# Gates' weights scaled once, router logits from the transposed halves, a third FFN tile ahead: one change to a recurrent block with experts

## What is computed

```python
xn = _layernorm(x, axis=-1)
# _L0_attn_ref(xn):
h = _rmsnorm(xn, pre_norm_w)
a = sigmoid(h @ w_a + decay_bias)
i_gate = sigmoid(h @ w_i)
v = h @ w_v
input_signal = sqrt(clip(1.0 - a * a, 1e-08)) * (i_gate * v)
rec_out = _chunked_scan(a, input_signal)      # state = a * state + signal along the sequence
x1 = xn + rec_out @ out_proj_w
gate, up = split(_rmsnorm(x1, ffn_norm_w) @ w_gate_up, 2, axis=-1)
attn = x1 + silu(gate) * up @ w_down
# _L0_ffn_ref(xn): logits = xn @ w_router, the best two of 8 experts per token,
# softmax over the two, y = square(relu(xn @ w_fc[e])) @ w_proj[e], weighted sum
out = x + attn + moe
```

## Time and profile before

| | us |
|---|---|
| median of 3 runs (312.35 to 313.71) | 312.52 |
| profiled execution, its own time | 313.96 |
| span of the profiled execution, first to last instruction | 312.2 |
| TensorE busy | 288.3 (92%) |
| VectorE busy | 194.6 (62%) |
| ScalarE busy | 174.7 (56%) |
| GpSimd busy | 145.6 (47%) |

### The profile page before, as it was taken

How to read it: one execution, slowest core, us unless ns; L and a number is a source line. 1 busy time by engine, 2 the same in 40 slices (tenths; PEclk the granted TensorE clock), 3 DMA queues, 4 the chain that set the end, 5 groups by cost and what they waited for, 6 DMA issues and landing times.

```text
span 312.2 us, 5645 instructions
## 1 busy us (share of the span) xinstructions
PE 288.3 (92%) x1842; PEld 255.1 (82%) x1842; DVE 194.6 (62%) x467; ACT 174.7 (56%) x360; POOL 145.6 (47%) x129
## 2 busy tenths in 40 slices
PE   5599799997999969999998999899999999799993
PEld 5578688886898949889997989789988999688882
DVE  2486998799867767874555588645546555612323
ACT  2587596798657744553657545346566555423220
POOL 4633001003174013576686678656766666637400
PEclk9799979998999999999999999999999999979999
DMA  7999940005996000244344434243444444539998
GB/s 225 325 381 378 457 174 0 0 2 149 205 200 131 0 11 26 46 64 74 62 71 68 59 64 68 54 70 52 70 69 70 68 69 57 66 34 134 195 197 285
DMA packets 33356, 36.92 MB, mean 118 GB/s; under 512 B 5168, under 2 KB 30512, under 8 KB 33296
## 3 DMA queue, kind: packets, MB, share of 16 engines
q0 software_dynamic: 13840, 17.20, 34.8%
q1 hardware_dynamic: 16560, 17.25, 16.3%
q10 hardware_dynamic: 2928, 2.10, 2.1%
HBM read 24.68 MB, written 13.96 MB: 124 GB/s over the span
## 4 chain that ended last, share of the span: by engine, by line
PE 74%; DVE 10%; ACT 8%; issue 4%; DMA 2%; SPq 0%; DVEq 0%; ACTq 0%
PE ps L364 61%; PE ps L425 5%; PE ps L571 5%; DMA Waiv_raw<-in_L_attn_w_v_dram 2%; ACT h L735 2%; DVE at_lane L1068 1%; PE ps L373 1%; PE ps L390 1%; DVE gu L1109 1%; DVE h2T_lo L986 1%; DVE hT_lo L937 1%; ACT Wpj_hi L670 1%; ACT h2T_hi L743 1%; DVE X L1122 1%; DVE Wpj_lo L1104 1%
## 5 line engine op out<-in xcount | busy, mean ns | idle before, releaser
L1339 POOL DMA_INDIRECT xg<-xh_dram,gather_u x39 | 46.2, 1185 | 56.7 <-DVE picks L1139 47.5
L1348 POOL DMA_INDIRECT acc_dram<-yb,gather_u x39 | 62.4, 1599 | 16.0 <-issue 8.6
L364 PE MATMUL ps<-h2T_lo,Wgu_hi 128*128 128x512 f32 x128 | 43.5, 400 | 0.0
L364 PE MATMUL ps<-h2T_hi,Wgu_hi 128*128 128x512 f32 x128 | 41.6, 407 | 1.0 <-DVE h2T_lo L986 1.0
L1109 DVE TENSOR_TENSOR gu<-gu,ps 128x512 f32<-128x512 f32 x32 | 21.9, 684 | 29.8 <-PE ps L364 28.5
L364 PE MATMUL ps<-h2T_hi,Wgu_lo 128*128 128x512 f32 x128 | 40.3, 396 | 0.0
L364 PE MATMUL ps<-Wd_hi,guT_hi 128*128 128x256 f32 x128 | 36.6, 286 | 3.2 <-DVE guT_lo L1114 3.2
L364 PE MATMUL ps<-Wd_hi,guT_lo 128*128 128x256 f32 x128 | 36.5, 285 | 0.0
L364 PE MATMUL ps<-Wd_lo,guT_hi 128*128 128x256 f32 x128 | 36.4, 285 | 0.0
L755 ACT ACTIVATE gu<-ps 128x512 f32<-128x512 f32 x32 | 19.1, 596 | 29.3 <-PE ps L364 28.5
L1156 DVE TENSOR_TENSOR aT_lo<-ps,aT_hi 128x256 fp32r<-128x256 f32 x39 | 16.5, 424 | 28.5 <-ACT aT_hi L785 24.1
(11 more groups left out here) (173 smaller groups left out, 664.7 us busy)
## 6 DMA issues: line engine op xcount, KB each, us to landing
X<-acc_dram POOLq DMA_DIRECT2D x8, 512.0 KB, 10.6
acc_dram<-zero SPq DMA_DIRECT2D x1, 2176.0 KB, 15.7
X<-in_L_attn_x_dram SPq DMA_DIRECT2D x4, 512.0 KB, 8.1
Wgu_raw<-in_L_attn_w_gate_up_dram SPq DMA_DIRECT2D x4, 512.0 KB, 10.0
xh_dram<-X ACTq DMA_DIRECT2D x4, 512.0 KB, 7.6
Wfc_raw<-in_L_ffn_w_fc_dram SPq DMA_DIRECT2D x4, 512.0 KB, 12.2
Wpj_raw<-in_L_ffn_w_proj_dram SPq DMA_DIRECT2D x4, 512.0 KB, 4.9
out_dram<-X SPq DMA_DIRECT2D x3, 512.0 KB, 5.6
```

Source lines behind the costliest of these rows:

```text
L364: return nc.tensor.matmul(dst, lhs, rhs, start=start, stop=stop, skip_group_check=group)
L1339: pool.indirect_dma_start(out=xg[i % XG][:, :], out_offset=None, in_=xh_dram, in_offset=bass.IndirectOffsetOnAxis(ap=gather_u[:, i:i + 1], ...
L1348: pool.indirect_dma_start(out=acc_dram[i % 2], in_=yb[i % YB][:, :], in_offset=None, compute_op=ALU.add, out_offset=bass.IndirectOffsetOnA ...
```

## The change

1. `pre_w` goes into the gates' weights. GpSimd's `scale_gates(n)` multiplies each of the three raw weights by `pre_w` in place, before ScalarE takes the high half. `split_h` then splits the transposed rows unscaled, so `hT` is the normalised sequence itself.
2. `copy_xh` and `xhT` are gone. The router's weights are split too (`Wr_two`, hi beside lo, 16 columns), and `logits` runs four small products per tile of 128 tokens on the halves: `hT` hi with both halves of the weights, `hT` lo with the high one. `take_logits` on VectorE adds the two columns of partial sums.
3. The small loads are issued before the wait for the constants. `normalise_x(0)` is shared: ScalarE takes tiles 0 and 1, VectorE 2 and 3, and it comes before the weights' halves. `transpose_x` goes tile by tile.
4. `aiv` takes the products in the order hi·hi, hi·lo of the weights, then lo of `hT`, with a wait ahead of each; the first gate no longer waits for all weights.
5. The lists are reordered: `logits` lies between other sequences' gates, `transpose_x(1)` comes after `logits(0)`.
6. FFN tile 2 gets banks 6 and 7 and is made right after `aiv(3, 5)`, ahead of `down(0)`. VectorE's `weights_lo(5)`, `lanes(2)`, `lanes(3)` move back, the weights' halves of the experts move forward by one or two places, and `weights_lo(15)`, `weights_lo(16)` come before d = 8.

```diff
         def gu_bank(d):
+            if d == 2:
+                return 6
...
             def transpose_x(c):
                 pe.wait_ge(xh_ready[c], 1)
                 if c:
-                    pe.wait_ge(xhT_copied, c)
-                transpose_tokens(X[c], TX, xT_done)
+                    pe.wait_ge(hT_split, K * c)
+                for j in range(J):
+                    if c == 0 and j == J // 2:
+                        pe.wait_ge(xh_half, 1)
+                    for k in range(K):
+                        last = nc.tensor.transpose(ps[:, TX + k, j * P:(j + 1) * P], X[c][:, j, k * P:(k + 1) * P],
+                                                   ident[:, :])
...
             def logits(c):
-                pe.wait_ge(xhT_copied, c + 1)
+                pe.wait_ge(hT_split, K * (c + 1))
                 if c == 0:
-                    pe.wait_ge(router_loaded, 16)
+                    pe.wait_ge(wr_split, 1)
...
-                        last = nc.tensor.matmul(ps[:, LOGIT, t * E:(t + 1) * E], xhT[c % 2][:, k, j * P:(j + 1) * P],
-                                                Wr[:, k, :], start=k == 0, stop=k == K - 1)
+                        rows_hi, rows_lo = (hT[c][h][:, k, j * P:(j + 1) * P] for h in range(2))
+                        product(ps[:, LOGIT, t * 2 * E:(t + 1) * 2 * E], rows_hi,
+                                Wr_two[:, k, :, :].rearrange("p h e -> p (h e)"), k == 0, False, True)
+                        last = product(ps[:, LOGIT, t * 2 * E:t * 2 * E + E], rows_lo, Wr_two[:, k, 0, :],
+                                       False, k == K - 1, True)
...
             def aiv(b, n):
                 if n == 0:
-                    pe.wait_ge(hT_split, K * (b + 1))
-                    if b == 0:
-                        pe.wait_ge(w_lo, 3)
+                    pe.wait_ge(hT_hi, K * (b + 1))
...
-                for m, (l, h) in enumerate(PRODUCTS):
+                for m, (l, h) in enumerate(((0, 0), (1, 0), (0, 1))):
+                    if b == 0 and m == 0 and r == 0:
+                        pe.wait_ge(w_hi, what + 1)
+                    if b == 0 and m == 1 and r == 0:
+                        pe.wait_ge(w_lo, what + 1)
+                    if n == 0 and m == 2:
+                        pe.wait_ge(hT_split, K * (b + 1))
...
-            keep_clock(56, 7)
+            keep_clock(64, 7)
             transpose_x(0)
-            keep_clock(24, 7)
+            keep_clock(20, 7)
             aiv(0, 0)
             aiv(0, 1)
-            transpose_x(1)
             aiv(0, 2)
             aiv(0, 3)
             logits(0)
+            transpose_x(1)
...
             transpose_x(3)
+            aiv(1, 2)
             logits(2)
-            aiv(1, 2)
+            aiv(1, 3)
             logits(3)
-            aiv(1, 3)
...
             for d in range(FIRST):
-                gate_up(d, 0)
-                gate_up(d, 1)
+                if d != 2:
+                    gate_up(d, 0)
+                    gate_up(d, 1)
                 if d == 1:
                     aiv(3, 5)
+                    gate_up(2, 0)
+                    gate_up(2, 1)
...
+            def scale_gates(n):
+                pool.wait_ge(w_loaded[n], 16)
+                raw = pieces[n][1][2]
+                G.tensor_tensor(raw, raw, pre_w[:, :, None].to_broadcast([P, K, D]), ALU.mult).then_inc(w_scaled, 1)
...
             root_x(0)
-            for n in range(3):
-                weights_lo(n)
-            for c in range(1, B):
-                root_x(c)
+            pool.wait_ge(pre_loaded, 16)
+            scale_gates(0)
+            scale_gates(1)
+            gates_lo(0)
+            scale_gates(2)
+            root_x(1)
+            gates_lo(1)
+            gates_lo(2)
+            root_x(2)
+            root_x(3)
```

More of the change, by code:

```diff
@@ L146, in recurrent_moe_block @@
                 put(f"guT{u}_lo", [P, S], F32R, guT_at + 4 * KB * u + 2 * KB)) for u in range(2)]
-        xhT = [put(f"xhT{u}", [P, K, S], F32, guT_at + 4 * KB * u) for u in range(2)]
         moe_at = room(20 * KB - 256)
@@ L675, in normalise_x @@
                 act.wait_ge(rstd_ready, c + 1)
-                for j in range(J):
+                for j in range(J // 2 if c == 0 else J):
                     t = J * c + j
@@ L847, in _ @@
             gate(1)
+            split_gu(1)
             weights_hi(7)
-            split_gu(1)
             gate(2)
@@ L877, in _ @@
                         block_in(i)
-                        if v == 0 and d > FIRST:
+                        if v == 0:
                             split_gu(d - 1)
@@ L927, in normalise_x @@
                 dve.wait_ge(rstd_ready, c + 1)
-                for j in range(J):
+                for j in range(J // 2 if c == 0 else 0, J):
                     t = J * c + j
@@ L931, in normalise_x @@
                                            ALU.subtract, ALU.mult)
[L932 removed]
+                last.then_inc(xh_half if c == 0 else xh_ready[c], 1)
             def split_h(c):
@@ L991, in take_logits @@
                 dve.wait_ge(logit_done, B)
-                ins = V.tensor_copy(logit[:, :, :], ps[:, LOGIT, 0:T * E].rearrange("p (t e) -> p t e", e=E))
-                ins.then_inc(logit_copied, 1)
+                two = ps[:, LOGIT, 0:2 * T * E].rearrange("p (t h e) -> p t h e", h=2, e=E)
+                chain.step(V.tensor_copy(logit[:, :, :], two[:, :, 1, :]))
+                V.tensor_tensor(logit[:, :, :], logit[:, :, :], two[:, :, 0, :], ALU.add).then_inc(logit_copied, 1)
             def top_two():
@@ L1170, in _ @@
             normalise_x(2)
+            gated_value(0, 0)
             split_h(1)
-            normalise_x(3)
+            gated_value(0, 1)
             scales()
-            gated_value(0, 0)
-            gated_value(0, 1)
-            split_h(2)
             signal(0, 0)
             signal(0, 1)
+            split_h(2)
             cumulate(0, 0)
             recur(0, 0)
+            cumulate(0, 1)
             split_h(3)
-            cumulate(0, 1)
             recur(0, 1)
@@ L1205, in _ @@
             lanes(1)
-            lanes(2)
-            lanes(3)
             up(0)
             gated_value(3, 1)
+            lanes(2)
             split_gu(0)
             up(1)
+            lanes(3)
+            split_gu(1)
             cumulate(1, 0)
-            split_gu(1)
             recur(1, 0)
```

108 lines of the change are left out of this document (55 added, 53 removed).

## The result

The changed kernel takes 308.88 us in the median of 20 runs (306.99 to 310.15); 20 runs of the kernel before made beside them gave 311.54 us (308.9 to 314.67). The ratio is 0.9922, 95% interval 0.9897 to 0.9948; the ratios compare undisturbed runs and so leave the longest runs of the kernel before out, which is why they come nearer to 1 than the medians do. Over all runs of this study that have a granted clock beside them, 57 of before and 26 of after, the medians are 312.45 and 309.01 us. The profiled execution has a span of 307.3 us (before 312.2) at a clock of 0.986, and its own time is 309.08.

A forecast was written before the change was run, and what follows sets the result against it. TensorE, busy 288 of 312.2 us, was taken as the bound, so time could come only from its idle and slow pieces. 2.6 + 0.3 + 0.6 + 1.1 = 4.6 us took the median from 312.52 to 307.9 us, range 305.9 to 310.3.

The forecast's parts named there:

- Start, 2.6 us: Up to the first gate: normalising first and less TensorE idling end `aiv(0, 0)` at 14.8 instead of 17.4, 2.6 us ahead.
- rival B: Start gives little: dear GpSimd scalings, later sequence 0 or lower clock, each taking 1.5 to 3 us; 309.5 to 311, chance 0.2.
- case E: Start: table load runs early after all, but lo of `hT` still waits for VectorE; 0.3 us better, 307.6, inside the forecast.
- 16 to 42 us, 0.3: Gates to first projection: VectorE's chain sets the pace, projection at 39.6 instead of 42.55, lead 2.9 us, 0.3 more.
- no change: 16 to 42 us: `logits(c)` keeps 16 weight loads of 128 columns, which paced it, so its time stays.
- I leave this as it is: First projection: stays at the lower clock, 4.94 us for 16, as the wait and small logits ahead of it remain.
- rival A: Clock stays up behind the projection, VectorE not hit elsewhere: 0.8 us at 42 to 46; 306 to 307, chance 0.2.
- 59 to 92 us, 0.6: First FFN tiles: `down(0)` 3.7 us earlier, but waits for VectorE leave 0.6 us at `down(3)`.
- paid by VectorE's waits: Lower-clock stretch at 76 to 79 us: its cost was counted as covered by TensorE's waits for VectorE.
- 92 to 117 us, 1.1: Expert start: first block 0.55 us earlier, the second block's wait of 1.16 us gone; 1.1 us more.
- Rival D: Slower: more stretches at 1.2 GHz behind six short idle pieces, 1.7 us each, up to 316.4 us; chance 0.03.
- Before has four such stretches. I count on one fewer: TensorE's clock: of four stretches at 1.2 GHz in the kernel before, the start's was expected to go.

The follow-up runs named there:

- table_early: The changed kernel plus a 128 x 1 ScalarE copy behind its wait for the constants, so the table load runs under sequence 0's load; 307.84 us.
- after_again: The changed kernel once more, unaltered, as reference on the same chip for edits of it; 309.13 us.
- pre_alone: The changed kernel with only `pre_w`'s load issued first, the other two small loads after the wait for the constants; 309.42 us.

## Why the prediction was right, and where it was not

The forecast, 307.9 us with 305.9 to 310.3, faster, holds the measured 308.88. The saving of 4.6 us was put 1.2 to 1.9 too high (2.7 between the medians of the first 20 runs of each kernel, 3.4 over all), and the base, 312.52 from three runs, lay 1.0 above the 20. That the sum fits is in part luck, as the steps show:

- **Start, 2.6 us: mis-sized, 0.9 to 2.1.** The gate was forecast at 13.4 and began at 14.89, at 13.80 in the profiles with a full clock there. `aiv(0, 0)` ended 0.9 us ahead of before, not 2.6. Three terms were off. Sequence 0 came 1.1 us late, not 0.4 (my end was 1). The transposes were taken at the full clock (1.10) and took 1.54, the dummies 2.34 where I had 1.6: the lower level, which I had only in rival B. And I gave VectorE's two tiles no price: beside GpSimd's scaling they took 2.15 us; they stayed hidden under the table load, but held the second half of the transposes in `table_early`. Of my case E's 0.3 us nothing was left at the projection. The 1.28 us for the table load was right; a drain behind it does not show here either (9.02 + 1.28, next activation at 10.31). The scaling, priced by the subtraction at 1.24, took 1.04, and TensorE did not wait 1 us for any low half.
- **16 to 42 us, 0.3: 1.2.** The VectorE chain had 0.5 us of wait ahead of the last logits, not 1.0. Without the lower level at the start the projection came at 39.18 to 39.20; I had said 39.6. The logits stayed 0.11 us per product, "no change", as said.
- **Behind the projection** my "I leave this as it is" was one draw of two: the full clock in the first profile (rival A's 0.8 us, in fact 1.2), the lower one in `after_again` and `pre_alone`.
- **59 to 92 us, 0.6: the number by luck.** `down(0)` went without a wait, and `down(1)` to `down(3)` waited 0.64, 1.09 and 0.72 us for `guT_lo`, with 0.7, 1.1 and 1.1 said; the lead went from 3.4 to 4.0 at `down(3)`. But before's stretch at 76 to 79 was not "paid by VectorE's waits": with the start of `down(0)` at 75.16 and 75.12, projection 2 came at 91.68 with it and at 90.09 without. So 1.6 us of the lead are the stretch, and VectorE takes back more than all that tile 2 gives: without the stretch the term is a loss of 1.0.
- **92 to 117 us, 1.1: 1.5.** The first block's wait is 0.97, the second's is gone.
- **Rival D** (more stretches): the opposite came. The changed kernel idles in shorter pieces and loses 3.2 us by the clock, not 5.7.
- **The step that failed is the account of the clock**: I counted the stretches of one execution as fixed costs at fixed places, "Before has four such stretches. I count on one fewer". They are draws: by their clocks the runs of before lost 1.8 to 9.7 us, those of after 0.6 to 4.6, where one stretch loses 1.7. My sum of places came out in the first profile (5.4 us ahead at block 2 against 4.6), but there before had three stretches up to block 2 and after one; with the same ones it is 2.2. The medians moved by 2.7 to 3.4 us. At the same clock the change as built is worth 1.6 us (1.2 to 1.9), and the place of the small loads took back 1 to 1.3 us of what the head gives. Why the changed kernel falls to the lower level less often is not shown; in the one place where it can be seen, near 75 us, two of three profiles with the wait of 2 us have the stretch and none of ten without that wait.

## What to carry to other kernels

Before a term is read off a stretch at the lower clock, look at the granted clocks of several runs: they come in steps of one stretch, and a saving can be a matter of how often it falls. Compare places in profiles that have the same stretches, or distances between two places with none between them: a step that seemed to give 0.6 us cost 1.0. Idle pieces ahead of dense work are where stretches followed; whether filling one pays has to be measured over many runs. Don't issue small loads of single values together with the transfer that everything waits for, and don't let GpSimd work on large tiles beside VectorE's normalising: a later issue cured both here, for 1 to 1.3 us at the same clock.
